# Order of TensorE's products in a Winograd FFN: the first and the last inner tile

## What is computed

```
x = x + attention_a(layernorm(x))     # gated linear attention in chunks of 128
x = x + ffn(layernorm(x))             # F1
x = x + attention_b(layernorm(x))     # softmax attention
x = x + ffn(layernorm(x))             # F2, same weights as F1

ffn(x): gate = silu(x @ Wg.T); up = x @ Wu.T; return (gate * up) @ Wd.T
        W = (codes - 128) * scale per row; hidden width 1408
```

## Time and profile before

| | us |
|---|---|
| median of 3 runs (lowest to highest) | 982.57 (982.09 to 983.09) |
| profiled execution, device time | 982.55 |
| its span, first to last instruction | 980.8 |
| TensorE busy in the span | 960.1 |
| first matmul of blocks 0, 1, 2, 3 | 266.10, 378.99, 759.15, 869.49 |

### The profile page before, as it was taken

How to read it: one execution, slowest core, us unless ns; L and a number is a source line. 1 busy time by engine, 2 the same in 40 slices (tenths; PEclk the granted TensorE clock), 3 DMA queues, 4 the chain that set the end, 5 groups by cost and what they waited for, 6 DMA issues and landing times.

```text
span 980.8 us, 12989 instructions
## 1 busy us (share of the span) xinstructions
PE 960.1 (98%) x4798; PEld 544.6 (56%) x4818; DVE 585.6 (60%) x1096; ACT 406.3 (41%) x790; POOL 431.3 (44%) x444
## 2 busy tenths in 40 slices
PE   6999999999999999999999999999999999999998
PEld 4888878887734444444444445544455444444443
DVE  7565766859767676776343443524455676766643
ACT  4332223345577544664222212222144665446630
POOL 5543525388456665665300000000133466655565
PEclk9999999999999999999999999999999999999999
DMA  9200300014120000000000000000000000110001
GB/s 325 118 1 1 119 1 1 2 43 130 32 98 1 1 1 0 1 1 1 1 1 1 1 1 1 1 1 1 1 1 1 1 1 1 44 43 0 1 14 73
DMA packets 12302, 26.05 MB, mean 27 GB/s; under 512 B 1744, under 2 KB 1744, under 8 KB 12240
## 3 DMA queue, kind: packets, MB, share of 16 engines
q1 hardware_dynamic: 12240, 25.22, 7.2%
HBM read 21.02 MB, written 4.19 MB: 26 GB/s over the span
## 4 chain that ended last, share of the span: by engine, by line
PE 81%; DVE 8%; POOL 4%; issue 4%; ACT 2%; DMA 1%; SPq 0%; POOLq 0%; DVEq 0%; ACTq 0%
PE psum L1805 53%; PE psum L2030 12%; PE psum L2032 12%; PE psum L2157 1%; POOL yt L810 1%; PE psum L1827 1%; POOL hid L769 1%; DVE xq L1250 1%; DVE xn L1227 1%; DVE yt L1613 1%; DMA wqk_raw<-wk 1%; PE psum L1838 1%; DVE wv_lo L1281 1%; DVE xres L1395 1%; DVE state L1382 1%
## 5 line engine op out<-in xcount | busy, mean ns | idle before, releaser
L773 POOL TENSOR_TENSOR hid<-hid,hid_hi 128x512 f32<-128x512 f32 x88 | 102.7, 1167 | 96.8 <-DVE hid_hi L1547 96.8
L2030 PE MATMUL psum<-xf,w_gu 128*128 128x512 f16 x352 | 133.8, 380 | 0.6 <-DVE gate L1512 0.6
L2030 PE MATMUL psum<-xf,w_s 128*128 128x512 f16 x264 | 100.0, 379 | 2.6 <-DVE up L1520 1.4
L2032 PE MATMUL psum<-xf,w_gu 128*128 128x512 f16 x264 | 100.1, 379 | 0.0
L624 POOL TENSOR_TENSOR xrstd<-xvar,minus_half 128x1 f32<-128x1 f32 x32 | 17.5, 562 | 122.9 <-DVE xvar L1221 122.9
L1034 ACT ACTIVATE hid_lo<-hid 128x512 f16<-128x512 f32 x88 | 54.9, 624 | 34.2 <-POOL hid L773 34.2
L2032 PE MATMUL psum<-xq,w_s 128*128 128x512 f16 x176 | 66.7, 379 | 0.0
L769 POOL TENSOR_TENSOR hid<-up,gate 128x512 f32<-128x512 f32 x44 | 55.9, 1271 | 23.1 <-ACT gate L1029 23.1
L2030 PEld LDWEIGHTS psum<-xf,w_gu 128*128 128x128 f16 x352 | 34.3, 98 | 55.4 <-ACT acc L1019 15.5
L1029 ACT ACTIVATE gate<-gate,sg_xs 128x512 f32<-128x512 f32 x44 | 31.7, 721 | 63.7 <-DVE gate L1530 63.6
L1547 DVE TENSOR_SCALAR hid_hi<-hid 128x512 f16<-128x512 f32 x88 | 37.5, 427 | 32.0 <-POOL hid L769 30.5
(11 more groups left out here) (284 smaller groups left out, 2415.7 us busy)
## 6 DMA issues: line engine op xcount, KB each, us to landing
out<-xres SPq DMA_DIRECT2D x16, 256.0 KB, 2.0
xres<-x SPq DMA_DIRECT2D x3, 1024.0 KB, 13.2
codes_gu<-gateT SPq DMA_DIRECT2D x1, 2816.0 KB, 17.0
codes_gu<-upT SPq DMA_DIRECT2D x1, 2816.0 KB, 9.7
codes_da<-downT SPq DMA_DIRECT2D x1, 1536.0 KB, 6.8
codes_db<-downT SPq DMA_DIRECT2D x1, 1280.0 KB, 10.0
xres<-x SPq DMA_DIRECT2D x4, 256.0 KB, 3.0
wqk_raw<-wk SPq DMA_DIRECT2D x1, 1024.0 KB, 6.9
```

The costliest lines, as they stand in the source:

```text
L773: nc.gpsimd.tensor_tensor(hid[:, :], hid[:, :], hid_part(hid_hi, j, half), ALU.subtract).then_inc(rest_done, 1)
L2030: nc.tensor.matmul(bank(use[0]), w, x_operand(piece, k, False), start=start and k == 0, stop=False, skip_group_check=not start)
L2032: last = nc.tensor.matmul(bank(use[0]), w, x_operand(piece, k, True), start=False, stop=k == 1, skip_group_check=not start)
```

## The change

```diff
@@ ffn, TensorE's program @@
                     if j > 0:
                         part(7, j - 1, alpha(j - 1, 2), False)
+                    if j == 0:
+                        part(5, j, delta(j, 0), True)
                     part(6, j, alpha(j, 1), False)
                     if j > 0:
                         part(4, j - 1, alpha(j - 1, 3), False)
-                    part(5, j, delta(j, 0), True)
-                    if j > 0:
+                        part(5, j, delta(j, 0), True)
                         part(3, j - 1, delta(j - 1, 1), False)
                 j = JT - 1
                 most = range(j)
@@
                 down(0, down_lo(0), hid_lo, most)
                 part(4, j, alpha(j, 3), False)
+                down(0, down_hi(0), hid_hi, most)
                 part(3, j, delta(j, 1), False)
-                down(0, down_hi(0), hid_hi, most)
                 down(1, down_lo(1), hid_lo, most)
                 down(1, down_hi(1), hid_hi, most)
```

## The result

| | before | after |
|---|---|---|
| median of 12 runs each (lowest to highest), us | 982.57 (982.03 to 983.24) | 984.79 (984.24 to 986.05) |
| span of the profiled execution, us | 980.8 | 983.2 |
| mean granted clock of TensorE | 0.999 | 1.000 |

The ratio is 1.0024, with a 95% interval from 1.0016 to 1.0032. The change costs 2.22 us, where the sum had been +2.01 and the forecast 984.5. It lies just above the bound of 0.2% (1.97 us), and the interval spans that bound. One execution of one kernel further down (the first-tile edit in blocks 1 to 3) took 2029.47 us, twice as long as its other nine, for a cause that nothing here shows; that kernel's ratio is made without it.

What follows compares the result with a forecast made beforehand. TensorE, busy 98% of the span, was taken to bound the kernel. Terms 0.86 - 0.07 + 0.36 + 0.31 + 0.33 + 0.22 gave +2.01 us on 982.55, so 984.5 us, range 982.8 to 985.6.

Steps and rivals of the forecast that it cites:

- the sum: Whole kernel: the terms of both edits added up to +2.01 us; chance 0.55.
- Block 0's first tile, +0.86: Piece 5 still waits for VectorE's read of bank 3, and piece 6's four matmuls come behind it: +0.86 us.
- some 0.24: Block 0's first tile: piece 6's loss before the change, waiting for ScalarE's copy of piece 1, some 0.24 us.
- Blocks 1 to 3's first tiles, -0.07: Piece 5 first fills a wait in block 2, -0.07 us; blocks 1 and 3 change by 0.
- The last tiles: Moving piece 3 makes `hid_lo` delay `y_low`: +0.36, +0.31, +0.33 and +0.22 us in blocks 0 to 3.
- +0.31: Block 1's last tile: low downs of `t` = 2 wait for `y_low`, starting at 458.03 against 457.72, +0.31 us.
- Within 0.2%: Whole kernel: a measured time within 0.2% (1.97 us) of the kernel before; chance 0.54.
- Not slower: Last tile: piece 3's wait won in full if `hid_lo` starts 0.8 us sooner; 981.8 or 980.7 us, chance 0.12.
- More than counted: Moved chains meet other POOL work, one pairing changes for the worse: +1.07 us more, 985.6 us; chance 0.15.
- the clock fall: Block 0's longer idle stretch drops TensorE to 1.2 GHz for one tile: +6 us, 990.6 us; chance 0.01.

Runs made afterwards that it cites:

- The run with the other bank: Piece 5 ahead of piece 6 at the first tile, block 0's sum of squares in bank 1, against the kernel before: 982.13 us against 982.62.
- the one with the bank alone: Block 0's sum of squares in bank 1 instead of bank 3, order of pieces unchanged, against the kernel before: 982.85 us against 982.86.
- three downs: Only three high down products ahead of piece 3 at the last tile, rest as in the kernel before: 981.32 us against 982.86.
- twenty downs: Twenty down products ahead of piece 3 at the last tile, rest as in the kernel before: 992.69 us against 982.86.

## Why the prediction was right

**Block 0's first tile, +0.86.** Right within the 0.02 that the rounding leaves, and by the step given: piece 5 was already held, as the late weight load at 269.85 showed, though the view of waits names no wait there. The run with the other bank shows the cause, the one with the bank alone that the wait had been filled. One number of the working was too small: piece 6 lost 0.39 and not "some 0.24". The step took the end of the small products' record, 268.78, for the earliest start of what follows; what follows can start 0.81 behind their start, 0.14 before that end. It did not enter the sum, because both orders are bound by piece 5, which starts at the same time in either; it did make the expectation for bank 1 too small, -0.3 for a measured -0.5.

**Blocks 1 to 3's first tiles, -0.07.** -0.08, and nothing else above 0.03.

**The last tiles.** +0.36, +0.33 and +0.22 came out as +0.36, +0.33 and +0.21. The mis-sized term is block 1's, "+0.31", which was +0.22. `y_low` started at 457.30 in before's time (459.02 less 1.72), as worked out, but the low downs followed its end more closely. After, TensorE and ScalarE in block 1, beside the earlier trace rows:

```profile
458.66 0.60 PE L1827 MATMUL psum<-ident,xn 128*128 128x128 f32 x4
459.66 0.60 PE L1805 MATMUL psum<-wd_a,hid_lo 128*128 128x512 bf16 x2 [0.40 <-ACT y_low L1058]
```

```profile
459.02 1.07 ACT L1058 ACTIVATE y_low<-psum 128x512 f32<-128x512 f32 x2
```

The step added a `y_low` of 0.60 and the hand-over of 0.14 from block 0's first tile. Two take 1.07, and one that starts right behind another instruction and has no second behind it takes 0.58, as this one in block 0:

```profile
354.96 0.58 ACT L1058 ACTIVATE y_low<-psum 128x512 f32<-128x512 f32 x1
```

So the first of the two ends near 459.60, and the hand-over was 0.06.

**Not in the sum.** The 0.50 ahead of block 0. Over the traces of all twelve kernels, whose code is the same up to there, block 0 starts anywhere from 265.78 to 267.25. It is a property of the execution and not of the change, and the medians average over it. That the median came within 0.21 us of the sum is no test as fine as that: its interval reaches 0.8 us to each side, and what confirms the terms is the balance of the traces, +1.91. "Within 0.2%" had the largest chance because the sum of +2.01 lay on the bound; the measured 2.22 lies above it by less than its own interval.

**The rivals.** "Not slower" named the right point: `hid_lo` would have had to start 0.8 us sooner. It never came closer to piece 3 (5.87 us, with three downs as with ten); with three downs piece 3 itself starts 1.51 us sooner, and that gives the gain. "More than counted" did not come: VectorE's `add_y` took 1.74 us after as before. Nor did the clock fall in the changed kernel. The window around the new idle stretch (PE, PEld, DVE, ACT, POOL busy, clock, DMA share, GB/s):

```profile
268.00:272.00 4.00, 2.90 (x19) 1.87 (x18) 0.91 (x3) 2.11 (x3) 0.55 (x1) 1.00 0.90 309
```

TensorE stood still for 1.1 us in it and was granted 1.00, the 2.4 GHz level. The Trainium skill ("TensorE: Matmul & The Clock Gate", A second HAM failure mode) says that frequent small idle times between groups of matmuls, with PSUM banks used in turn, made the clock swing in a kernel. The changed kernel shows no such thing. The kernel with twenty downs shows one fall, between 844.5 and 848.2 us, behind three idle stretches of 0.7, 0.64 and 0.21 us; the same three left the clock at 1.00 in block 0, and so did one of 2.6 us in block 3. That is a single fall and no swing, and it doesn't settle the rule. The prediction's one per cent was for a fall in the changed kernel; its price of 0.216 us for each 512-column matmul at the lower level is near what the one fall shows (five matmuls in 2.27 us for 1.25).

## What to carry to other kernels

Work that is put into a wait should be as long as the wait: three matmuls into 0.43 us gave all of it, ten gave a loss, since what was put behind them is late by the rest and stands in other engines' queues ahead of work that was on time. Before two pieces change places, look at what each would wait for alone; a wait that another piece fills is in no list of waits, but its weight load stands off its usual place. Where a step hangs on a bank that holds something unrelated, the order can only be won together with the bank.

## What was not expected of the hardware

The hand-over between engines is not one number. From ScalarE's end to TensorE's start it was 0.14 us at block 0's first tile and 0.06 behind `y_low` in block 1. And the start of block 0, behind 266 us of one and the same code, moved by 1.5 us between executions, while the stretches behind it that no edit touched repeated to within 0.03 us, except behind the fall of the clock with twenty downs. That fall is the other thing: one and the same pattern of short waits and transposes kept the clock at 1.00 in block 0 and was followed by 1.2 GHz in block 2.
